# An attention-mixed 1x1 convolution: another opening and another end, and matmuls on a tile of ones up to the first product

## The reference

```
v = group_norm(x)                                   # mean, variance over 16 channels x 3136 pixels
h = relu(batch_norm(mean(v, pixels) @ fc_w.T))      # 32 values per image
ch_att = sigmoid(h @ ch_w.T + ch_b)                 # 512
fl_att = sigmoid(h @ fl_w.T + fl_b)                 # 512
kn_att = softmax(h @ kn_w.T + kn_b)                 # 4
agg_w  = sum_k kn_att[k] * weight[k]                # 512 x 512, another one for each image
y      = agg_w @ (v * ch_att)
out    = x + batch_norm(y * fl_att)
```

## Time and profile before

| | us |
|---|---|
| median of 3 runs (lowest, highest) | 2108.76 (2107.36, 2108.93) |
| the profiled execution: its own time | 2107.46 |
| the profiled execution: span of its trace | 2105.7 |
| PE busy | 2047.6 |
| DVE busy | 1909.7 |
| ACT busy | 1726.7 |

### The profile page before, as it was taken

One profiled execution on the slowest core, in us unless ns is written; L12 is line 12 of the kernel. 1 busy time (PEld: TensorE's weight loads), 2 busy tenths in 40 slices (PEclk: granted clock), 3 DMA queues, 4 the chain that ended last, 5 costly groups with the idle time before them and its releaser, 6 DMA issues.

```text
span 2105.7 us, 33303 instructions
## 1 busy us (share of the span) xinstructions
PE 2047.6 (97%) x10820; PEld 1058.4 (50%) x10820; DVE 1909.7 (91%) x3079; ACT 1726.7 (82%) x2295; POOL 0.2 (0%) x4
## 2 busy tenths in 40 slices
PE   0999999999999999999999999999999999999998
PEld 0455555555555555555555555555555555555554
DVE  7999999999999999999999999999999999999973
ACT  4788888888888888888888888888888888888885
POOL 0000000000000000000000000000000000000000
PEclk9999999999999999999999999999999999999999
DMA  9465556565556565556655565665565655566522
GB/s 333 134 210 199 199 189 207 206 209 196 196 200 206 195 209 199 202 192 209 209 196 205 191 206 196 209 206 194 192 209 202 208 200 192 196 206 207 175 105 105
DMA packets 237284, 415.99 MB, mean 198 GB/s; under 512 B 7248, under 2 KB 236624, under 8 KB 236752
## 3 DMA queue, kind: packets, MB, share of 16 engines
q1 hardware_dynamic: 237264, 415.74, 57.8%
HBM read 210.19 MB, written 205.52 MB: 197 GB/s over the span
## 4 chain that ended last, share of the span: by engine, by line
PE 97%; DVE 1%; DMA 1%; ACT 1%; SPq 0%; issue 0%; DVEq 0%
PE product L696 32%; PE product L695 32%; PE product L697 32%; DMA x_ring<-x 1%; DVE mixed_weight L557 0%; PE small L668 0%; DVE chunk_stats L354 0%; SPq L198 0%; DVE w_lo L573 0%; ACT y L295 0%; ACT x_norm L232 0%; DVE x_lo L362 0%; ACT x_hi L241 0%; ACT w_hi L308 0%; DVE x_ring L368 0%
## 5 line engine op out<-in xcount | busy, mean ns | idle before, releaser
L695 PE MATMUL product<-x_hi,w_hi 128*128 128x448 f16 x3584 | 1264.7, 353 | 6.7 <-DVE x_lo L362 3.6
L696 PE MATMUL product<-x_lo,w_hi 128*128 128x448 f16 x3584 | 1264.8, 353 | 0.0
L697 PE MATMUL product<-x_hi,w_lo 128*128 128x448 f16 x3584 | 1264.5, 353 | 0.0
L250 ACT ACTIVATE y<-product,out_bias,out_scale 128x448 f32<-128x448 f32 x896 | 641.8, 716 | 260.6 <-PE product L697 254.8
L232 ACT ACTIVATE x_norm<-x_ring,norm_bias,norm_scale 128x448 f32<-128x448 f32 x896 | 671.0, 749 | 1.4 <-DVE norm_bias L435 1.4
L368 DVE TENSOR_TENSOR x_ring<-x_ring,y 128x896 f32<-128x896 f32 x448 | 480.7, 1084 | 92.0 <-ACT y L250 86.0
L695 PEld LDWEIGHTS product<-x_hi,w_hi 128*128 128x128 f16 x3584 | 353.5, 99 | 335.3 <-issue 10.5
L697 PEld LDWEIGHTS product<-x_hi,w_lo 128*128 128x128 f16 x3584 | 351.1, 98 | 328.2 <-issue 1.6
L696 PEld LDWEIGHTS product<-x_lo,w_hi 128*128 128x128 f16 x3584 | 351.0, 98 | 322.4 <-issue 1.3
L354 DVE BATCH_NORM_STATS2 chunk_stats<-x_ring 128x6 f32<-128x448 f32 x896 | 492.8, 613 | 3.7 <-DMA x_ring<-x 1.2
L362 DVE TENSOR_TENSOR x_lo<-x_norm,x_hi 128x1792 f16<-128x1792 f32 x224 | 451.8, 2017 | 13.1 <-ACT x_hi L241 11.4
(11 more groups left out here) (69 smaller groups left out, 257.6 us busy)
## 6 DMA issues: line engine op xcount, KB each, us to landing
x_ring<-x SPq DMA_DIRECT2D x224, 896.0 KB, 4.8
out<-x_ring SPq DMA_DIRECT2D x224, 896.0 KB, 3.9
weight<-wt SPq DMA_DIRECT2D x4, 1024.0 KB, 15.1
params<-par SPq DMA_DIRECT2D x1, 462.0 KB, 3.4
```

The source lines that it names most:

```text
L250: nc.scalar.activation(y[:, s % 2, t], acc[k % BANKS][:, 0:COLS], ACT.Identity, bias=obias[:, t:t + 1], scale=oscale[:, u, t:t + 1]).then_ ...
L695: nc.tensor.matmul(bank, whi[:, u, t, cols], hi, start=(t == 0), stop=False)
L696: nc.tensor.matmul(bank, whi[:, u, t, cols], lo, start=False, stop=False)
L697: ins = nc.tensor.matmul(bank, wlo[:, u, t, cols], hi, start=False, stop=(t == CT - 1))
```

## The change

The order of the loads: seven chunks, params, the weights in eight halves, then seven chunks. POOL makes the batch norm constants, with ACT's two activations. ACT sums the absolute values by halves (`top`) as they land. DVE takes no statistics of image 1 in the opening. `x_hi` of chunks 0 and 1 is made from x in one step (`first_hi`), ahead of `x_norm`; DVE makes the float32 value of chunk 0 (`first_norm`) and its `x_lo` after all the weights. PE takes the high passes (x_hi with w_hi and with w_lo) of seven of the eight output tiles of chunks 0 and 1 first, waiting for each channel tile alone, and the passes with `x_lo` after that (`first_products`). PE's matmuls on `ones` (22 ahead of the two tiny matmuls, 6 behind them) write PSUM bank 6, which a product overwrites.

The first turn is written out ahead of the loop. In it the adds of chunks 0 to 5 are 12 accumulating DMAs (SBUF to SBUF) that POOL issues; statistics and attentions of image 1 stand later than in the other turns (`early`). At the end ACT puts the bias into the last slot of the ring ahead, DVE multiplies the last four output tiles out of PSUM and adds them in one instruction each, and each is stored by itself.

```diff
+        xhi0 = whi[:, 1].rearrange("p t c -> p (t c)")[:, 0:CT * COLS].rearrange("p (t n) -> p t n", t=CT)
+        xlo0 = wlo[:, 1].rearrange("p t c -> p (t c)")[:, 0:CT * COLS].rearrange("p (t n) -> p t n", t=CT)
+        xn0 = y[:, 1]
+        awake = ones[:, :].bitcast(f16)
...
         NORM_AHEAD, SPLIT_AHEAD = 2, 1
+        EARLY_ADDS = 6
...
-            sp.dma_start(pa[:, :], par).then_inc(params_in, 16)
             for slot in range(RING):
-                if slot == CHUNKS + 2:
-                    for k in range(KERNELS):
-                        sp.dma_start(w[:, k], wt[:, k]).then_inc(weight_in[k], 16)
+                if slot == CHUNKS:
+                    sp.dma_start(pa[:, :], par).then_inc(params_in, 16)
+                    for j in range(2 * KERNELS):
+                        k, half = divmod(j, 2)
+                        two = slice(half * CT // 2, (half + 1) * CT // 2)
+                        sp.dma_start(w[:, k, two], wt[:, k, two]).then_inc(weight_in[j], 16)
...
+                    if first and s < EARLY_ADDS:
+                        for h in range(2):
+                            sp.wait_ge(half_in[h], 16 * (s + 1))
+                    else:
+                        sp.wait_ge(add_done, turn.at(2 * RING, 4 + 2 * (s + 1)))
                     sp.dma_start(out_d[b, :, :, n * COLS:(n + 1) * COLS], xs[:, s]).then_inc(chunk_out[s], 16)
...
+            body(0, False, True)
+            with sp.Fori(1, TURNS - 1) as i:
...
+            for t in range(CT):
+                sp.wait_ge(tail_done[t], 1)
+                sp.dma_start(out_d[B - 1, :, t, (CHUNKS - 1) * COLS:], xs[:, RING - 1, t]).then_inc(tail_out[t], 16)
...
+                if first and s < 2 + EARLY_ADDS:
+                    if s >= 2 and t % 2 == 0:
+                        act.wait_ge(half_in[t // 2], 16 * (s - 1))
...
+            def top(j):
+                k, half = divmod(j, 2)
+                two = slice(half * CT // 2, (half + 1) * CT // 2)
+                act.wait_ge(weight_in[j], 16)
+                if j > 2:
+                    act.wait_ge(abs_done, j - 2)
+                room = y_free[:, j % 3 * HALF_W:(j % 3 + 1) * HALF_W].rearrange("p (t n) -> p t n", n=C)
+                nc.scalar.activation(room, w[:, k, two], ACT.Abs, accum_out=wsum[:, j:j + 1]).then_inc(abs_done, 1)
...
+            def first_hi(s, t):
...
+                nc.scalar.activation(xhi0[:, t] if s == 0 else xhi[:, 1, t], xs[:, s, t], ACT.Identity,
+                                     bias=nbias[:, 0, t:t + 1], scale=nscale[:, 0, t:t + 1]).then_inc(first_hi_ready, 1)
...
+            def mix_first(o):
+                cols = slice(o * P, (o + 1) * P)
+                if o == 1:
+                    act.wait_ge(att_ready, 1)
+                nc.scalar.activation(mix[:, :, cols], w[:, 0, :, cols], ACT.Copy,
+                                     scale=katt[:, 0:1]).then_inc(first_mix0_ready, 1)
...
+            def weight_hi(o):
+                cols = slice(o * P, (o + 1) * P)
+                if o == 0:
+                    act.wait_ge(catt_ready, 1)
+                act.wait_ge(first_mix_ready, o + 1)
+                for t in range(CT):
+                    nc.scalar.activation(whi[:, 0, t, cols], mix[:, t, cols], ACT.Copy,
+                                         scale=catt[:, t:t + 1]).then_inc(first_whi_ready, 1)
...
+            top(0)
+            top(1)
             guess(start, 0)
+            for j in range(2, 6):
+                top(j)
+            first_hi(0, 0)
+            exponentials(start, 0)
+            top(6)
+            top(7)
+            for t in range(1, CT):
+                first_hi(0, t)
+            mix_first(1)
+            weight_hi(0)
+            mix_first(2)
+            first_hi(1, 0)
+            first_hi(1, 1)
+            weight_hi(1)
+            first_hi(1, 2)
+            first_hi(1, 3)
+            mix_first(3)
+            weight_hi(2)
+            norm(start, 1, 0, True)
+            norm(start, 1, 1, True)
+            weight_hi(3)
+            norm(start, 1, 2, True)
+            norm(start, 1, 3, True)
...
+                norm(start, 2, t, True)
+            split(start, 2)
...
+                        if last and s == RING - 2:
+                            nc.scalar.activation(xs[:, s + 1, t], xs[:, s + 1, t], ACT.Identity,
+                                                 bias=obias[:, t:t + 1]).then_inc(tail_biased, 1)
...
             group_mean(start, 0)
-            for t in range(CT):
-                stats(start, CHUNKS, t)
             group_var(start, 0)
...
             norms(start, 0)
-            stats(start, CHUNKS + 1, 1)
-            stats(start, CHUNKS + 1, 2)
+            dve.wait_ge(bn_ready, 1)
             logits(start, 0)
-            stats(start, CHUNKS + 1, 3)
             attentions(start, 0)
-            split(start, 0)
...
...
+            def first_norm(t):
+                nc.vector.tensor_scalar(xn0[:, t], xs[:, 0, t], nscale[:, 0, t:t + 1], nbias[:, 0, t:t + 1],
+                                        ALU.mult, ALU.add).then_inc(xn0_ready, 1)
...
+            dve.wait_ge(att_ready, 1)
+            for half in range(2):
+                dve.wait_ge(weight_in[half], 16)
+            step(nc.vector.tensor_scalar(mix[:, :, 0:P], w[:, 0, :, 0:P], katt[:, 0:1], None, ALU.mult))
+            add_kernel(0, 1)
+            dve.wait_ge(abs_done, 2 * KERNELS)
             nc.vector.reduce_sum(wsum1[:, :], wsum[:, :], AX.X).then_inc(wsum_ready, 1)
+            add_kernel(0, 2)
             dve.wait_ge(top_moved, 1)
             nc.vector.reduce_max(wtop[:, :], top_row, AX.X).then_inc(wtop_ready, 1)
+            add_kernel(0, 3)
             dve.wait_ge(top_moved, 2)
...
+            add_kernel(1, 1)
...
+            first_split(0)
+            add_kernel(1, 2)
+            add_kernel(1, 3)
+            add_kernel(2, 1)
+            first_split(1)
+            add_kernel(2, 2)
+            add_kernel(2, 3)
+            add_kernel(3, 1)
+            first_split(2)
+            add_kernel(3, 2)
+            add_kernel(3, 3)
+            first_norm(0)
+            first_norm(1)
+            first_split(3)
+            first_norm(2)
+            first_norm(3)
+            dve.wait_ge(xn0_ready, CT)
+            dve.wait_ge(first_hi_ready, CT)
+            nc.vector.tensor_tensor(xlo0, xn0, xhi0, ALU.subtract).then_inc(lo_ready, 1)
+            dve.wait_ge(first_hi_ready, 2 * CT)
+            dve.wait_ge(xn_ready, 2)
+            nc.vector.tensor_tensor(xlo[:, 1], xn[:, 1], xhi[:, 1], ALU.subtract).then_inc(lo_ready, 1)
+            dve.sem_inc(wlo_ready, 1)
+            split(start, 2)
...
+                whole = {(0, 0): 7, (0, 1): 8, (0, 2): 9, (0, 3): 10, (2, 2): 11, (2, 3): 12, (3, 0): 13,
+                         (6, 1): 14, (6, 2): 15, (6, 3): 16}
...
+                early = {"means": (3, 1), "mean": (3, 1), "var": (3, 1), "norms": (4, 0), "logits": (4, 2),
+                         "att": (4, 3), "mix": [(5, 0), (5, 1), (5, 2)], "split": {(6, 0): (0, 1, 2, 3)}}
+                usual = {"means": (2, 0), "mean": (2, 1), "var": (3, 0), "norms": (3, 1), "logits": (3, 3),
+                         "att": (4, 1), "mix": [(4, 2), (5, 0), (5, 1)], "split": {(5, 3): (0, 1), (6, 0): (2, 3)}}
...
+                        if t == 0 and s and not (first and s - 1 < EARLY_ADDS):
                             add(turn, s - 1, 1)
...
+                for t in range(CT):
+                    k = CT * (RING - 1) + t
+                    dve.wait_ge(tail_biased, t + 1)
+                    dve.wait_ge(mm_done, turn.at(4 * RING, k + 1))
+                    nc.vector.scalar_tensor_tensor(out=xs[:, RING - 1, t], in0=acc[k % BANKS][:, 0:COLS],
+                                                   scalar=oscale[:, 1, t:t + 1], in1=xs[:, RING - 1, t],
+                                                   op0=ALU.mult, op1=ALU.add).then_inc(tail_done[t], 1)
...
+            pool.wait_ge(params_in, 16)
+            nc.gpsimd.tensor_scalar(v_all[:, :], pa[:, where["bn_v"][0]:where["abn_v"][1]], BN_EPS, None,
+                                    ALU.add).then_inc(bn_vars_ready, 1)
+            pool.wait_ge(bn_guess_ready, 2)
...
+            def add(s, half):
+                pool.wait_ge(evac_done, BANKS + 4 * s + 2 * half + 2)
+                if s:
+                    pool.wait_ge(half_in[half], 16 * s)
+                two = slice(2 * half, 2 * half + 2)
+                pool.dma_start(xs[:, s, two], y[:, s % 2, two], accum_op=ALU.add).then_inc(half_in[half], 16)
+            for s in range(EARLY_ADDS):
+                for half in range(2):
+                    add(s, half)
...
+            def keep_awake(n):
+                for _ in range(n):
+                    nc.tensor.matmul(acc[BANKS - 1][:, 0:2 * P], awake[:, 0:P], awake[:, :], start=True, stop=True)
...
             nc.tensor.matmul(top_row, wsum1[:, 0:1], p_("ident"), start=True, stop=True).then_inc(top_moved, 1)
```

(34 more changed lines are left out.)

237 lines of the change are left out of this document (127 added, 110 removed).

## The result

The changed kernel takes 2102.84 us (median of 8 runs, 2100.22 to 2103.95), beside 2108.22 for the kernel before (2107.36 to 2108.93): a ratio of 0.9974, interval 0.9965 to 0.9983. So 5.4 us were won where I had forecast 14.7, and the time lies outside the range of 2089 to 2100. The profiled execution took 2103.30 us, with a span of 2101.4.

A forecast was written before the change was run, and what follows sets the result against it. PE was taken as the bound, 97% of the chain with no gap in the middle, leaving only the two ends. 14.9 - 3.1 + 2.9 = 14.7 us won gave a forecast of 2093.5 us, range 2089 to 2100.

The forecast's parts named there:

- The step that failed: First turn: the 12 accumulating DMAs cost 0 up to 9 us each, judged by a store's 3.9 us to landing.
- Rival (c): Accumulating DMAs over 9.12 us each delay chunks 0 to 5; at 11.6 us the gain is gone; chance 0.06.
- The opening: Kernel start: first product at 38.3, low passes at 53.0, chunk 2 at 60.6 instead of 75.5, 14.9 us won.
- POOL's constants: Opening: eight batch norm steps on POOL from 21.1 end by 28.4, hidden; cost taken as 0, bounded by 3 us.
- The half-weight pass on ACT: Opening: ACT's pass over 1024 columns takes 1.2 us, under the 1.38 between two landings.
- What is late next: After the opening: PE waits 1.7 us for chunk 7 and 1.4 more at chunk 8, together 3.1, bounds 0 and 5.
- Then DVE catches up: After chunk 8: DVE makes up its lateness, so the waits at chunks 7 and 8 stay at 3.1 us together.
- rival (a): Chunks 7 and 8: DVE's order costs nothing, so 17.8 us are won and the time is 2090.4; chance 0.2.
- The matmuls on ones: Opening: 28 extra matmuls hide in PE's waits; they cost nothing and are given no gain.
- rival (b): After PE's short waits, eight matmuls at half pace cost 1.5 us each time; 2099 with POOL late by one; chance 0.2.
- The end: Last evacuation, add and store: 3.2 us instead of 6.2, 2.9 won, or 1.2 if a store takes 4.3 whatever its size.

The follow-up runs named there:

- the kernel with copies: The changed kernel with POOL's twelve accumulating DMAs made plain copies over the ring's slots, so the output of chunks 0 to 5 of image 0 lacks x: 2089.74 us.
- the kernel with a timely ring: Three chunks added by accumulating DMAs, three by DVE, statistics later in DVE's order: without the matmuls on ones 2091.89 us, with them 2091.47.
- the later order: Changed kernel with chunks 0 to 2 added by accumulating DMAs, 3 to 5 by DVE, and statistics of chunks 14 to 19 later in DVE's order: 2091.47 us.

## Why the prediction was wrong

**The step that failed** is "The 12 accumulating DMAs have no row. The nearest is a store of twice the size, 3.9 us to landing ... Cost 0". I asked one question of them: does ACT get its half back in time? It does; ACT never waits for `half_in`. But I priced the DMA as a latency with one customer, and it is work for sixteen engines that stores and loads need too. Measured: 13.1 us between the changed kernel and the same with copies. This one term is more than the whole miss of 9.3; the rest of the forecast was 3.8 us too slow.

Rival (c) named the right suspect, and its rule was wrong: it let the DMAs decide only from D over 9.12 us, by the chain of halves. They landed in 7.5 in the median, under that bound (the slowest took 11.3), ACT never waited for them, and they cost 13 us all the same by way of the stores, SP's waits and the ring. It also made them decide only for a kernel slower than before. Its cited mechanism (DVE keeps POOL from writing descriptors) isn't needed: the issues on POOL take 0.85 to 1.03 us throughout.

**The opening** was right and 2.1 us too slow. First product 37.44 for 38.3; low passes 50.91 for 53.0; chunk 2 58.49 for 60.6; 17.0 won for 14.9. DVE's row from 38 to 51 holds what was listed, each a little shorter: `first_norm` 0.93 for two where I had 0.55 each, an output tile's four splits 1.13 for 1.16.

**POOL's constants** were hidden: nine steps of 0.20 to 0.31 us, with a wait for ACT between, from 21.47 to 24.73, well ahead of the 28.4 at which DVE needs them. The half-weight pass on ACT took 1.04 to 1.06 where I had 1.2.

**What is late next** was right for chunk 7 (1.36 for 1.7). At chunk 8 the 0.97 of the kernel with copies answers to the 1.4 of the forecast, which had nothing for the ring. Together 2.3 for 3.1, or 2.6 by the distances of starts. "Then DVE catches up" holds only if the ring is in time, which I had not looked at: I never asked who else waits for what the new DMAs slow down.

**The sum without that one term**: 17.0 - 2.3 + 3.1 = 17.8 won from 2107.46 gives 2089.7 (with 2.6, 2090.0), and the kernel with copies took 2089.74. So the steps add up, and rival (a)'s 2090.4 is near what the schedule alone would have given.

**The matmuls on ones** cost PE nothing, as forecast; that they also gain nothing is confirmed only for the kernel with a timely ring. In the changed one the first ten matmuls of the product run 0.37 apart in spite of them, and DVE hides it, as I had said.

**The clock** (rival (b)): in the changed kernel's first profile 2.9 us were lost once, behind the 6.91, and nothing at the short waits. Its second profile lost 1.6 behind the 2.86 and 2.4 behind the 5.41, and the later order 1.7 behind a 2.50. So the rival's 1.5 for a short wait does occur, but not at each. That its 2099 was the nearest of the times above mine is luck.

**The end**: 3.06 us for 3.2 and, alone, 2.7 won for 2.9. Right.

## What to carry to other kernels

A DMA without a row is to be priced twice: by its landing, for the one who waits for it, and by its share of the DMA engines, for all others; then ask which transfers run beside it and who hangs on those. An idle engine is not free help: an add moved to DMA took the stores' time, moved to POOL it took DVE's, and the best of these kernels was a mixture, three of six chunks by DMA with the statistics later in DVE's order (2091.47 us, 16.3 less than before).
A loop that stores, waits and reloads hands each lateness on and catches up slowly: in the changed kernel, once the accumulating DMAs are over, a store behind a load takes 7.6 to 7.8 us of the 9.12 that a chunk has.
